# K's high part one slot later on ScalarE, its low part one slot later on VectorE

## The chip, the cores and the metric

The kernel runs on one core of one Trainium2 chip, in one launch. The metric is the device time of that core in microseconds. The kernel before takes 1835.96 us (median of 3 runs, 1834.97 to 1836.04).

## The reference

Inputs are x (16 batches of 512 rows by 512), a context of 16 x 512 x 1024, a length for each batch, two scalar gates, a bias row, and the weights of eight experts. All is fp32. Cut to what matters:

```
k, v  = split(ctx, 2, axis=2)                      # each 16 x 512 x 512
q     = heads(layernorm(x), 16) * 32 ** -0.5       # 16 heads of 32
s     = einsum('bhqd,bhkd->bhqk', q, heads(k)) + b + mask by length
x     = x + tanh(g_xattn) * (softmax(s) @ heads(v))
h     = layernorm(x)
logit = cos(h, centroids) + h @ w_route            # 8 experts, the best 2 kept
x     = x + tanh(g_ffn) * sum_e gate_e * (gelu(h @ w1_e + b1_e) @ w2_e + b2_e)
```

## The kernel before

There are two parts. The attention, which the change touches, comes first and fills the span up to about 1270 us; the experts' blocks follow.

The attention is a loop over 64 groups, written out in full. A group is one batch and four of its heads (a batch is four groups, g = 0 to 3). The loop is a software pipeline: in step l several groups are under way at once, each in another stage. A step has 16 slots, s = 0 to 15, and each engine's program is an in-order list of what it does in slot 0, slot 1 and so on. Engines meet only at semaphores.

**What TensorE does in a slot.** First "QK" (line 899): one 128x512 tile of the logits of group l, into one of two banks. Then "M" (line 911): a tile of the same logits, turned, of group l+2, whose only use is the row maximum. In some slots more follows:
- slot 0 and slot 3: the transposes TQ and TK of Q and K of group l+3 (`turn_rows`, line 858);
- slots 5, 9 and 13, and slot 1 of the next step: four heads' products of probabilities with V (`values`, line 830). The one in slot 5 is the first product with V. Slot 2 of the next step: the row sums (line 844);
- slot 5, behind the product: the transposes MT of the maxima of group l+1 (line 866);
- slots 7 and 9: the transposes DT of the row sums and OT of the output of group l-1 (line 932);
- slots 10 and 14: XT and LG, for the router.

**What the others do.** ScalarE takes each QK bank with an exponential (line 755), one a slot; QK of slot s waits for the exponential of slot s-2. VectorE takes each M bank with a maximum (line 1167), one a slot; M of slot s waits for the maximum of slot s-2. GpSimd adds up probabilities.

**The two turn banks.** All transposes go into two PSUM banks, `psT[0]` and `psT[1]`, in a fixed order: list `TURNS` (line 110) numbers them, and even numbers use bank 0, odd ones bank 1. In a full step the order is TQ, SM (the row sums), TK, MT, DT, OT, XT, LG, so TQ, TK, DT and XT share one bank, and SM, MT, OT and LG the other. `put_turn` (line 371) makes TensorE wait until the former user of the bank is taken out, `take_turn` (line 377) makes the taker wait for the transposes.

**Q and K in two parts.** Q and K are split into a high part in the matmul's format and the remainder. For Q (side 0) and K (side 1) `evac_turned` (line 703, ScalarE, line 708) copies the turn bank to the high part; `lo_part` (line 1082, VectorE, line 1086) subtracts the high part from the bank, gives the low part and releases the bank. SyncE then places them: two copies of the high part and one of the low part for each side, 256 KB each (line 464), and behind them the turned maxima, after ScalarE has copied those in slot 6 (`take_maxima`, line 727; DMA line 527). TensorE waits for all of them in slot 0 of the next step.

Before the change, K's transposes TK stand in slot 3 on TensorE, the high part in slot 4 behind that slot's exponential, the low part in slot 5 behind that slot's maximum. In steps with g = 0 ScalarE also normalises Q of a later batch, in slots 7, 9, 12 and 14 (line 697).

Of the kernel before, what the change touches and what calls it, by code (L numbers as in the profile page):

```python
# [142 lines left out]
def flamingo_kernel(nc, x, ctx_in, lens, g_xattn, g_ffn, b_in, w1, b1, w2, b2, cent, w_route, out):  # L143
# [31 lines left out]
    with outer:  # L175
# [54 lines left out]
        with ExitStack() as ctx:  # L230
# [146 lines left out]
            def take_turn(eng, st, name, off=0):  # L377

                i, before = turn_of(st, name, off)
                eng.wait_ge(s_turn[i], before + 1)  # L380
                return psT[i], s_took[i]
# [59 lines left out]
            def prob_of(st, off, u):  # L441


                return prob[:, u if u >= 2 else (st.l + off + u) % 2, :, :]
# [227 lines left out]
            def _(act):  # L672
# [30 lines left out]
                def evac_turned(st, side):  # L703

                    if st.rnd is not None or st.l + 3 >= 1:
                        act.wait_ge(s_stk[side], st.count(48, 3, 0))
                    bank, took = take_turn(act, st, "TK" if side else "TQ")
                    act.activation(turnedH[:, side, :], bank[:, :], ACT.Copy).then_inc(s_full, 1)
# [25 lines left out]
                def step(st):  # L734
                    if st.l == -1:
                        take_maxima(st)
                        i, before = turn_of(st, "MT")
                        act.wait_ge(s_took[i], before + 1)
                        for t in range(2):
                            act.dma_start(stB[98 + t:99 + t, 0, :, :].bitcast(F32),  # L740
                                          mT[HG * t:HG * t + HG, :].bitcast(F32)).then_inc(s_md[0], 16)
                    for s in range(16):
                        u, j = s // 4, s % 4
                        if st.on(0):
                            if j == 0 and st.l >= 1:


                                act.wait_ge(s_pv, st.count(PV, -1, (2, 1, 3, NT)[u]))
                                if u in (0, 2):
                                    act.wait_ge(s_acc, st.count(ADDS, -1, ADDS if u else HG))  # L750
                                else:
                                    i, before = turn_of(st, "SM")
                                    act.wait_ge(s_turn[i], before + 1)
                            act.wait_ge(s_qk, st.count(16, 0, s + 1))
                            act.activation(prob_of(st, 0, u)[:, j, :], psS[j % 2][:, :], ACT.Exp).then_inc(s_exp, 1)  # L755
                        if s in (0, 4) and st.on(3):
                            evac_turned(st, s // 4)
                            if s == 4 and st.l < 0:
                                place_k(st)
                        if s == 6 and st.on(1) and st.l >= 0:  # L760
                            take_maxima(st)
                        if s in (0, 4) and st.l == G:
                            for e in ((0, 1), (2, 3))[s // 4]:
                                w2_hi(e)
                        if s == 2 and st.on(-1):

                            act.wait_ge(s_pv, st.count(PV, -1, NT))
                            if st.l >= 2:
                                b, before = turn_of(st, "OT", -1)
                                act.wait_ge(s_turn[b], before + 1)  # L770
                            act.activation(attT[:, :], psO[:, :], ACT.Copy).then_inc(s_out, 1)
                        if s == 3 and st.on(-1):
                            if st.l >= 2:
                                b, before = turn_of(st, "DT", -1)
                                act.wait_ge(s_turn[b], before + 1)
                            bank, took = take_turn(act, st, "SM")
                            act.activation(sumT[:, :], bank[:, :], ACT.Copy).then_inc(took, 1)
                        if s == 8 and st.on(-5) and st.l <= G:
                            normalise(st)
                        if s == 11 and st.on(-5) and st.l <= G:  # L780
                            bank, took = take_turn(act, st, "XT")
                            act.activation(xT[:, :, :].rearrange("p k t -> p (k t)"), bank[:, :], ACT.Copy).then_inc(took, 1)
                        if st.g() == 0 and s in (7, 9, 12, 14) and st.on(4):
                            normalise_q(st, (7, 9, 12, 14).index(s))
                        if s == 10 and st.g() == 1 and st.on(-6) and st.l <= G:
                            gate_exp(st)
# [212 lines left out]
            def _(dve):  # L999
# [151 lines left out]
                def step(st):  # L1151
# [9 lines left out]
                    for s in range(16):  # L1161
                        if st.on(2):

                            if s == 0 and st.l + 2 >= 1:
                                dve.wait_ge(s_nm, st.count(2, 2, 0))
                            dve.wait_ge(s_m, st.count(16, 2, s + 1))
                            dve.tensor_reduce(mx[:, s // 4, s % 4:s % 4 + 1], psM[s % 2][:, :], AX.X, ALU.max).then_inc(s_mx, 1)  # L1167
                        if s == 0 and st.on(-6) and st.l <= G:
                            route_logit(st, s)
                        if s in ((1, 2) if st.l == -1 else (1, 5)) and st.on(3) and st.l != -2:  # L1170
                            lo_part(st, int(s > 1))
                        if s in (5, 6, 12, 13, 14, 15) and st.g() == 1 and st.on(-6) and st.l <= G:
                            route(st, s)
                        late = 10 if st.l in (-2, -1) else 0
                        if st.g() in (2, 3) and s - late in (0, 3) and st.on(8 - st.g()):
                            stats(st, 2 * (st.g() - 2) + (s - late) // 3)
                        if st.g() in (2, 3) and s - late in (2, 4) and st.on(8 - st.g()):
                            aggregate(st, 2 * (st.g() - 2) + (s - late) // 4)
                        if s == 8 and st.on(-1):

                            bank, took = take_turn(dve, st, "DT")
                            sums = bank[:, :].rearrange("p (i h c) -> p i h c", i=NT, h=HG)[:, :, :, 0]
                            dve.reciprocal(rsum[:, :, :], sums).then_inc(took, 1)
                        if s == 10 and st.on(-1):

                            b, before = turn_of(st, "DT")
                            dve.wait_ge(s_took[b], before + 1)
                            i, before = turn_of(st, "OT")
                            dve.wait_ge(s_turn[i], before + 1)
                            each = rsum[:, :, :].rearrange("p i (h a) -> p (i h) a", a=1).to_broadcast([P, NT * HG, DH])  # L1190
                            heads = psT[i][:, :].rearrange("p (h c) -> p h c", c=DH)
                            dve.tensor_tensor(heads, heads, each, ALU.mult).then_inc(s_scaled, 1)
                        if s == 11 and st.on(-1):
                            g, par = st.g(-1), ((st.l - 1) // 4) % 2
                            if g == 0:
                                dve.wait_ge(s_res[par], st.bpair(16, -1, 16))
                            dve.wait_ge(s_scaled, st.count(1, -1, 1))
                            bank, took = take_turn(dve, st, "OT")
                            dst = xres[:, par, :, g * P:(g + 1) * P]
                            dve.scalar_tensor_tensor(out=dst, in0=bank[:, :].rearrange("p (i c) -> p i c", i=NT), scalar=tanh_a[:, 0:1],  # L1200
                                                     in1=dst, op0=ALU.mult, op1=ALU.add).then_inc(took, 1)
                        if s == 10 and st.g() == 1 and st.on(-5) and st.l <= G:
                            row_norms(st)
                        if s in (12, 13) and st.on(-1):
                            column_stats(st, 2 * (s - 12))
                        if s == 14 and st.g() == 0 and st.on(-4):
                            row_stats(st)
                        if s == 15 and st.on(-5) and st.l <= G:
                            route_logit(st, s)
# [449 lines left out]
```

## Time and profile before

| | |
|---|---|
| median of 3 runs | 1835.96 us |
| profiled execution: time, span | 1835.64 us, 1833.9 us |
| granted TensorE clock, mean of the span | 0.988 of full speed |
| TensorE matmul busy | 1732.6 us, 94% |
| VectorE busy | 1360.4 us, 74% |
| GpSimd busy | 1231.4 us, 67% |
| ScalarE busy | 1190.3 us, 65% |
| maxima on VectorE (line 1167) | 1024 of 690 ns |
| exponentials on ScalarE (line 755) | 1024 of 597 ns |
| QK (line 899), M (line 911) on TensorE | 1024 each, 467 and 416 ns |

"Busy" counts the time in which an engine has an instruction under way. Neighbouring instructions overlap a little in the records, so the distance from start to start is what an instruction costs its queue, and its own duration is what a waiting engine has to sit out. A row of the timeline gives the start, the duration, engine and line; "x3" is three instructions merged into one row; in brackets stands how long the engine was idle before and what ended the wait.

### The profile page before, as it was taken

Reading aid. Unit: us, or ns where it says so; the run is one execution under the profiler, and the core shown is the slowest. Engines: PE = TensorE matmul, PEld = TensorE weight load, DVE = VectorE, ACT = ScalarE, POOL = GpSimd, SP = SyncE. Lnnn points to the kernel's source line nnn. Section 1 sums busy time; section 2 is a strip of 40 time slices with the busy share of each in tenths; the row PEclk is TensorE's granted clock in tenths of the full one; section 3 lists DMA queues with packets and bytes.
Section 4 is the critical chain, followed back from the end, with each engine's and each line's share of the span. In section 5 each row is a group of like instructions: output and inputs, shape, how many; then the busy total and the mean of one; then the engine's idle time right before and its main releaser. Section 6 shows DMA issues by size and latency. Waiting matters only on the chain. (4 is left out here: it accounts for less than half of the span.)

```text
span 1833.9 us, 33174 instructions
## 1 busy us (share of the span) xinstructions
PE 1732.6 (94%) x9754; PEld 1047.6 (57%) x9755; DVE 1360.4 (74%) x3003; ACT 1190.3 (65%) x2049; POOL 1231.4 (67%) x1399
## 2 busy tenths in 40 slices
PE   2889999999999999999999999999699999999997
PEld 1344555555555555555554555554578778777886
DVE  5767888878888778788787877872566776767765
ACT  4457677676776767767677677766356666666664
POOL 1348567585775857757666676664568888888886
PEclk9999999999999999999999999999699999999999
DMA  7879899898998989989989897874458788887784
GB/s 156 143 133 188 163 172 187 128 214 146 171 185 130 210 150 171 186 128 206 155 164 191 138 199 106 182 128 144 143 121 170 152 161 159 177 156 150 155 165 74
DMA packets 173099, 291.45 MB, mean 159 GB/s; under 512 B 38014, under 2 KB 42110, under 8 KB 172976
## 3 DMA queue, kind: packets, MB, share of 16 engines
q1 hardware_dynamic: 138704, 219.88, 61.6%
q0 software_dynamic: 32960, 67.68, 18.7%
q10 hardware_dynamic: 1312, 2.38, 1.1%
q8 instruction: 61, 1.00, 0.3%
q14 instruction: 62, 0.51, 0.1%
HBM read 127.09 MB, written 71.63 MB: 108 GB/s over the span
## 5 line engine op out<-in xcount | busy, mean ns | idle before, releaser
L1167 DVE TENSOR_REDUCE bank<-bank 128x1 f32<-128x512 f32 x1024 | 695.9, 690 | 246.0 <-PE bank L911 237.8
L755 ACT ACTIVATE prob<-bank 128x512 f32<-128x512 f32 x1024 | 593.1, 597 | 363.7 <-PE bank L899 362.8
L659 POOL TENSOR_TENSOR prob<-prob 128x512 f32<-128x512 f32 x252 | 315.9, 1295 | 325.3 <-PE bank L830 325.3
L899 PE MATMUL bank<-stB,stack_a_then_w_hi 100*128 100x512 f32 x1024 | 476.9, 467 | 20.4 <-ACT prob L755 13.7
L911 PE MATMUL bank<-stack_a_then_w_hi,stB 98*128 98x512 f32 x1024 | 423.4, 416 | 23.5 <-DVE bank L1167 11.5
L899 PEld LDWEIGHTS bank<-stB,stack_a_then_w_hi 100*128 100x128 f32 x1024 | 193.5, 189 | 253.8 <-ACT prob L755 175.6
L663 POOL TENSOR_TENSOR prob<-prob 128x512 f32<-128x512 f32 x252 | 315.5, 1296 | 0.0
L830 PE MATMUL bank<-prob,vin 128*32 128x512 f32 x2048 | 273.6, 606 | 0.7 <-ACT prob L755 0.7
L1439 POOL DMA_INDIRECT out_dram<-yout,scatter_ids x144 | 227.7, 1581 | 52.5 <-issue 39.0
L911 PEld LDWEIGHTS bank<-stack_a_then_w_hi,stB 98*128 98x128 f32 x1024 | 198.1, 194 | 74.2 <-DVE bank L1167 42.2
L1412 POOL DMA_INDIRECT rows_in<-xn_rows,gather_ids x152 | 179.1, 1178 | 59.4 <-issue 44.3
L1373 PE MATMUL bankb<-turned_parts,w_parts 128*128 128x512 f32 x888 | 218.8, 402 | 0.0
L1373 PE MATMUL bankb<-stack_a_then_w_hi,gelu_parts 128*128 x576 | 198.8, 406 | 0.4
L1373 PEld LDWEIGHTS bankb<-turned_parts,w_parts 128*128 128x128 f32 x888 | 165.9, 190 | 37.8
L1545 ACT ACTIVATE yout<-out_with_bias,row_gates 128x512 f32<-128x512 f32 x144 | 92.3, 712 | 78.7 <-DVE out_with_bias L1619 68.0
L1565 DVE TENSOR_TENSOR turned_parts<-bankb,turned_parts 128x512 fp32r<-128x512 f32 x148 | 95.2, 684 | 54.2 <-ACT turned_parts L1525 48.0
L1373 PEld LDWEIGHTS bankb<-stack_a_then_w_hi,gelu_parts 128*128 128x128 f32 x576 | 108.2, 188 | 29.0 <-issue 4.8
L844 PE MATMUL bank<-prob,ones 128*32 128x512 f32 x1040 | 124.8, 598 | 0.0
L1373 PE MATMUL bankb<-regrouped_then_w,gelu_parts 128*128 x288 | 114.3, 397 | 0.0
L1525 ACT ACTIVATE turned_parts<-bankb 128x512 fp32r<-128x512 f32 x148 | 81.3, 596 | 40.5 <-PE bankb L1459 20.3
L1553 ACT ACTIVATE gelu<-bankb,b1s 128x512 f32<-128x512 f32 x74 | 50.9, 688 | 84.6 <-PE bankb L1373 65.4
L858 PE MATMUL bank<-ident,regrouped_then_w 128*128 128x128 f32 x512 | 81.0, 283 | 22.7 <-ACT regrouped_then_w L697 21.7
(205 smaller groups left out, 2177.5 us busy)
## 6 DMA issues: line engine op xcount, KB each, us to landing
stB<-regrouped_then_w SPq DMA_DIRECT2D x192, 256.0 KB, 5.7
stack_a_then_w_hi<-regrouped_then_w SPq DMA_DIRECT2D x183, 256.0 KB, 6.4
x_k_then_w<-in_x_dram SPq DMA_DIRECT2D x16, 1024.0 KB, 7.9
x_k_then_w<-in_ctx_dram SPq DMA_DIRECT2D x16, 1024.0 KB, 11.6
vin<-in_ctx_dram SPq DMA_DIRECT2D x16, 1024.0 KB, 8.4
xres<-in_x_dram SPq DMA_DIRECT2D x16, 1024.0 KB, 6.4
out_dram<-xres SPq DMA_DIRECT2D x16, 1024.0 KB, 7.4
xn_rows<-xn SPq DMA_DIRECT2D x60, 256.0 KB, 5.5
```

The source lines that it names most:

```text
L659: pool.tensor_tensor(first[:, j, :], first[:, j, :], more[:, j, :], ALU.add).then_inc(s_acc, 1)
L663: pool.tensor_tensor(first[:, j, :], first[:, j, :], then[:, j, :], ALU.add).then_inc(s_acc, 1)
L755: act.activation(prob_of(st, 0, u)[:, j, :], psS[j % 2][:, :], ACT.Exp).then_inc(s_exp, 1)
L830: last = pe.matmul(psO[DH * j:DH * (j + 1), :], vin[:, vpar, kt, c0:c0 + DH], p[:, j, :], start=(u == 0), stop=(u == NT - 1), skip_group_c ...
L844: last = pe.matmul(bank[DH * j:DH * (j + 1), :], ones[:, 0:DH], p[:, j, :], start=(u == 0), stop=(u == NT - 1), skip_group_check=True, til ...
L899: pe.matmul(psS[j % 2][:, :], stA[0:100, g, j, kt * P:(kt + 1) * P], stB[0:100, g, j, :], start=True, stop=True).then_inc(s_qk, 1)
L911: pe.matmul(psM[s % 2][:, :], stB[0:98, g, j, i * P:(i + 1) * P], stA[0:98, g, j, :], start=True, stop=True).then_inc(s_m, 1)
L1167: dve.tensor_reduce(mx[:, s // 4, s % 4:s % 4 + 1], psM[s % 2][:, :], AX.X, ALU.max).then_inc(s_mx, 1)
L1373: last = pe.matmul(bank, wts(p), mov(q), start=start and i == 0, stop=stop and i == 2)
L1412: pool.indirect_dma_start(rows[:, par, c, :], None, xn_d, bass.IndirectOffsetOnAxis(ap=gids[:, par, c:c + 1], axis=0), bounds_check=TOK - ...
L1439: pool.indirect_dma_start(out_rows, bass.IndirectOffsetOnAxis(ap=sids[:, h, c:c + 1], axis=0), yout[:, h, c, :], None, bounds_check=TOK - ...
L1565: dve.tensor_tensor(xTb[:, 1, k, :], bank_of(st, USE[k])[:, :], xTb[:, 0, k, :].bitcast(F32), ALU.subtract).then_inc(f_use, 1)
```

## The change

ScalarE's copy of K's high part goes from slot 4 to slot 5 and stands behind the exponential of slot 5. VectorE's subtraction for K's low part goes from slot 5 to slot 6 and stands behind the maximum of slot 6. In the steps before group 0, ScalarE's own DMAs for K move along with the copy. Nothing else moves: TensorE's, GpSimd's and SyncE's lists stay, and so do the order of the turn banks and all waits.

```diff
-                        if s in (0, 4) and st.on(3):
-                            evac_turned(st, s // 4)
-                            if s == 4 and st.l < 0:
+                        if s in (0, 5) and st.on(3):
+                            evac_turned(st, s // 5)
+                            if s == 5 and st.l < 0:
                                 place_k(st)
...
-                        if s in ((1, 2) if st.l == -1 else (1, 5)) and st.on(3) and st.l != -2:
+                        if s in ((1, 2) if st.l == -1 else (1, 6)) and st.on(3) and st.l != -2:
                             lo_part(st, int(s > 1))
```

## Rows read from the trace of the kernel before

**Rows 1.** Busy time by stage, the attention without its first two steps.
```profile
116.00:1270.00 1154.00, 1128.41 (x6797) 588.68 (x6800) 908.86 (x2107) 810.54 (x1471) 769.96 (x1040) 1.00 0.87 165
```

**Rows 2.** Groups of instructions by line, from 116 to 1215 us.
```profile
L899 PEld LDWEIGHTS bank<-stB,stack_a_then_w_hi 100*128 100x128 f32 x931 | 175.5, 189 | 218.9 <-ACT prob L755 154.3 <-issue 53.6
```

**Rows 3.** Timeline of TensorE, slots 6 to 9 of step 30 (g = 2).
```profile
649.30 0.48 PE L899 MATMUL bank<-stB,stack_a_then_w_hi 100*128 100x512 f32 x1
649.62 0.39 PE L911 MATMUL bank<-stack_a_then_w_hi,stB 98*128 98x512 f32 x1
649.85 0.39 PE L899 MATMUL bank<-stB,stack_a_then_w_hi 100*128 100x512 f32 x1
650.08 0.40 PE L911 MATMUL bank<-stack_a_then_w_hi,stB 98*128 98x512 f32 x1
650.32 0.60 PE L932 MATMUL bank<-ident,regrouped_then_w 128*128 128x128 f32 x4
650.67 0.48 PE L899 MATMUL bank<-stB,stack_a_then_w_hi 100*128 100x512 f32 x1
650.99 0.39 PE L911 MATMUL bank<-stack_a_then_w_hi,stB 98*128 98x512 f32 x1
651.41 0.50 PE L899 MATMUL bank<-stB,stack_a_then_w_hi 100*128 100x512 f32 x1
651.75 0.40 PE L911 MATMUL bank<-stack_a_then_w_hi,stB 98*128 98x512 f32 x1
652.08 0.64 PE L830 MATMUL bank<-prob,vin 128*32 128x512 f32 x4
```

**Rows 4.** Timeline of VectorE, slots 5 to 8 of the same step.
```profile
648.57 0.67 DVE L1167 TENSOR_REDUCE bank<-bank 128x1 f32<-128x512 f32 x1
649.14 0.68 DVE L1086 TENSOR_TENSOR regrouped_then_w<-bank,regrouped_then_w 128x512 fp32r<-128x512 f32 x1
650.05 2.07 DVE L1167 TENSOR_REDUCE bank<-bank 128x1 f32<-128x512 f32 x3 [0.23 <-PE bank L911]
```

**Rows 5.** Timeline of ScalarE, slots 4 to 8 of the same step.
```profile
647.92 0.59 ACT L708 ACTIVATE regrouped_then_w<-bank 128x512 fp32r<-128x512 f32 x1
648.40 0.60 ACT L755 ACTIVATE prob<-bank 128x512 f32<-128x512 f32 x1
649.82 0.60 ACT L755 ACTIVATE prob<-bank 128x512 f32<-128x512 f32 x1 [0.81 <-PE bank L899]
650.31 0.57 ACT L727 ACTIVATE regrouped_then_w<-bank 8x512 fp32r<-8x512 f32 x1
650.79 1.08 ACT L755 ACTIVATE prob<-bank 128x512 f32<-128x512 f32 x2
```

**Rows 6.** Timeline of TensorE, transposes OT of step 29 and QK behind them.
```profile
633.94 0.66 PE L932 MATMUL bank<-ident,regrouped_then_w 128*128 128x128 f32 x4
634.35 0.48 PE L899 MATMUL bank<-stB,stack_a_then_w_hi 100*128 100x512 f32 x1
```

**Rows 7.** Timeline of all engines, slots 7, 8 and 12 of step 28 (g = 0).
```profile
611.85 0.60 PE L932 MATMUL bank<-ident,regrouped_then_w 128*128 128x128 f32 x4
...
612.80 1.33 ACT L697 ACTIVATE regrouped_then_w<-x_k_then_w,q_shift,rstd 128x512 f32<-128x512 f32 x1
...
613.91 0.64 ACT L755 ACTIVATE prob<-bank 128x512 f32<-128x512 f32 x1
...
617.41 0.50 PE L899 MATMUL bank<-stB,stack_a_then_w_hi 100*128 100x512 f32 x1 [0.77 <-ACT prob L755]
```

**Rows 8.** Timeline of SyncE's DMA issues from slot 4 of step 30 on.
```profile
648.54 1.85 SPq L464 DMA_DIRECT2D stack_a_then_w_hi<-regrouped_then_w  x3
650.90 1.32 SPq L527 DMA_DIRECT2D stB<-regrouped_then_w  x2
...
659.50 1.13 SPq L502 DMA_DIRECT2D stack_a_then_w_hi<-bias_mask_rows  x4
```

**Rows 9.** DMA issues by size and median us to landing, 648.5 to 650.5 us.
```profile
stack_a_then_w_hi<-regrouped_then_w SPq DMA_DIRECT2D x3, 256.0 KB, 7.3
```

## The prediction

> **What bounds the kernel now.** I read the busy times by stage first. In the attention TensorE is busy 1128.41 of 1154 us, at a granted clock of 1.00, while VectorE has 908.86 and ScalarE 810.54 [rows 1]. So a step costs what TensorE's list costs, and the two engines that the change touches have room on average. The groups by line say where TensorE is held at all: the weight loads of QK sit idle 154.3 us in front of exponentials over 931 instructions, 0.17 us each [rows 2]. Last I read the timelines of one step, slot by slot, because the change is a matter of order and an average says nothing on that. Step 30 is a plain one (g = 2); its order and distances in slots 6 to 9 repeat from step to step, so it stands for the steps with g = 1, 2 and 3.
>
> In slots 6 to 9 TensorE runs QK, M, QK, M, DT, QK, M, QK, M, product [rows 3]. Up to DT the starts are 0.23 to 0.32 us apart: nothing holds it. DT starts at 650.32. The low part of K, which frees DT's bank, ran from 649.14 to 649.82 [rows 4], 0.50 us ahead. That half microsecond is all the cover there is.
>
> **What the ScalarE move does.** Before: exponential of slot 4, high part at 647.92, exponential of slot 5 at 648.40 [rows 5]. After: the exponential of slot 5 takes the place at about 647.92 and the high part follows at about 648.40 and ends at 648.99, 0.48 us later. The cost on ScalarE is nothing: the same two instructions in the other order, and the next exponential, of slot 6, waited 0.81 us for TensorE [rows 5]. The gain is nothing too: the earlier exponential releases QK of slot 7 only, which ran at 649.85 [rows 3], when the exponential had been done since 649.00 [rows 5]. No wait of TensorE in slots 4 to 7 goes.
>
> **What the VectorE move does.** The low part stood in a pause of VectorE: it ended at 649.82 and the maximum of slot 6 waited another 0.23 us for M [rows 4]. That maximum needs M of slot 6, so its start at 650.05 can't be earlier. The low part now queues behind it. From the row before, a subtraction starts 0.57 us after the maximum ahead of it (648.57 to 649.14), the three maxima in one row come 0.69 apart (2.07 / 3) [rows 4]; I take 0.60. Start 650.65, end 650.65 + 0.68 = 651.33. A release takes about 0.03 to 0.05 us more: the exponential of slot 7 ended at 650.79 + 0.60 = 651.39 and QK of slot 9, which waits for it, started at 651.41 [rows 3, 5]. DT therefore starts at about 651.38 and not 650.32: TensorE stands still for 1.06 us, in order, with QK of slot 8 and all that follows behind DT. Bounds: 1.03 with the 0.57, 1.17 with the 0.69 and the larger release.
>
> **What comes back in the same step.** From DT to the second product TensorE took 652.08 - 650.32 = 1.76 us. One gap in it is a wait: M of slot 8 to QK of slot 9 took 0.42 (650.99 to 651.41), for the exponential of slot 7, which stood behind the turned maxima at 650.31 [rows 3, 5]. After the stall that exponential is long done, so the two pairs run at 0.32 and 0.24 to 0.33. DT to QK is 0.35 when nothing held the transposes, and 0.41 where they start behind a pause [rows 3, 6]. I take 0.41 + 0.32 + 0.24 + 0.24 + 0.33 = 1.54, a return of 0.22 us. M of slot 9 now needs the maximum of slot 7, which follows the low part and ends near 651.23 + 0.69 = 651.92; M of slot 9 would start by TensorE's own list at 651.38 + 0.41 + 0.32 + 0.24 + 0.24 = 652.59, so that is not late. Net 1.06 - 0.22 = 0.84 us per plain step. Bounds: 0.70 (return of 0.33) and 1.17 (no return).
>
> Behind the second product ScalarE and VectorE have caught up in either kernel, so the rest of the step is the same, 0.84 us later, and nothing absorbs it.
>
> **Steps with g = 0.** There ScalarE is the one that is late: its normalising of Q runs from 612.80 for 1.33 us, the exponential of slot 8 starts at 613.91 behind it, and QK of slot 12 still waits 0.77 us for an exponential [rows 7]. With the stall DT starts at 611.85 + 1.06 = 612.91, QK of slot 8 at 613.32 and ends 0.48 later at 613.80, still ahead of 613.91. ScalarE's chain does not move, so the 0.84 us is given back by slot 12. I take 0 for these steps; the upper bound is the whole 0.84, if VectorE and not ScalarE sets the pace behind slot 9 once the low part has moved.
>
> **Transfers.** On SyncE the high parts are issued 0.48 us later, the low part once it is there, near 651.4, and the turned maxima behind it, near 652.0 and not 650.90. K's three copies needed 7.3 us to land [rows 8, 9]: from the last issue at about 649.8 that is 657.1, against the next step at 659.5 [rows 8]. With the low part 1.6 us later it lands at 658.7, against 659.5 + 0.84 = 660.3. That hides 1.6 us of slack and no more; I count 0. GpSimd's additions wait for exponentials and products that don't move and cost nothing.
>
> **The sum.** The stall needs a K in slot 6 (steps up to 60) and a DT in slot 7 (steps from 1): 60 steps. 15 of them have g = 0 (4, 8, ... 60), 45 don't. 45 x 0.84 + 15 x 0 = 37.8 us. The profiled execution took 1835.64 us, 0.32 below the median, so I compare with it: 1835.64 + 37.8 = 1873.4 us, slower by 2.1%.
>
> **The Trainium skill on the clock.** The granted clock is 1.00 over the stretch although TensorE idles for 1154 - 1128.41 = 25.6 us in it, some of it in waits of 0.77 us [rows 1, 7]. The Trainium skill (TensorE: Matmul & The Clock Gate, Part 1) says that the throttled state is the default and that activity is what releases it. By that, the added idle could cost clock as well as time; that case is a rival below, and without it the sum stands. No row of this kernel shows idle of 1 us per step bringing the clock down.
>
> **Rivals.**
> 1. The stall is there and the placed rows come too late on top, or the g = 0 steps don't give it back. The low part's slack of 1.6 us is for a step without bulk loads; with a megabyte load in the queue a landing could slip. For it: DMA busy share 0.87 [rows 1]. Against it: what is loaded in bulk is issued behind these rows in most steps. Price: the full 1.06 in all 60 steps, 63.6 us, 1899 us.
> 2. More comes back than I see, as the plain steps have waits for exponentials behind slot 9 too: 154.3 us over about 58 steps is 2.7 us per step [rows 2]. If a third of each stall is absorbed there and only 0.55 stays: 45 x 0.55 = 24.8, 1860 us. Against it: the pause of the second product empties both queues.
> 3. The other side, faster: the exponential of slot 5 runs 0.48 us earlier, and if the release of DT were not what K's low part holds, the chain of exponentials could run ahead. It would take away the wait in front of QK of slot 9, 0.42 - 0.24 = 0.18 us [rows 3], in 60 steps: 10.8 us, 1824.8 us. It decides if DT's bank is free by 650.32 and the exponential of slot 7 can start before 650.79; but the latter stands behind QK of slot 7 and the turned maxima, which don't move.
> 4. No change: the two turn banks are counted so that DT doesn't follow K's transposes in its bank. Then both moves are in cover, 1835.6 us. The order of the turns speaks against it: K's and DT's are two apart in every step.
> 5. The clock falls, as said above: a tenth of the stretch at 1.2 GHz would add up to 0.1 x 1128 = 113 us, 1986 us with the stall.
>
> **How the numbers follow.** Forecast (net 0.70 to 1.06 per plain step, small change in g = 0 steps: 1867 to 1888) 0.72; rival 1 0.11; rival 2 0.11; rival 3 0.02; rival 4 0.02; rival 5 0.02. The range that leaves out no more than 2 in 10 reaches a good way into rivals 1 and 2: 1860 to 1892. What a measurement of this kernel can tell from no change is about 0.2%, 3.7 us; rivals 1, 2 and 5 are slower with the forecast: slower 0.96, same 0.02, faster 0.02.
>
> **What would show it.** In the timeline of a plain step: the low part of K behind the maximum of slot 6, its start about 0.6 us after it; idle time of TensorE before DT (line 932), ended by VectorE's line 1086, near 1 us, where no such releaser stood before; about 60 of them, some 60 us in the list of waits. QK of slot 6 to DT 2.08 us instead of 1.02 [rows 3]; DT to the second product near 1.54 instead of 1.76. Plain steps 0.84 us longer, and the step with g = 0 as long as before. The waits of QK for exponentials should shrink by some 10 us in slot 9 and more in g = 0 steps. It is wrong if no wait stands in front of DT, if waits for DMA appear in slot 0, or if the granted clock leaves 1.00.

## The result and the profile after

The changed kernel takes 1880.21 us (median, 1878.3 to 1882.68) against 1835.47 us for the kernel before in the same session: ratio 1.0244, 95% interval 1.0231 to 1.0256, 44.7 us slower. 1873.4 us was forecast, in a range of 1860 to 1892. The profiled execution took 1879.62 us, its span 1877.9 against 1833.9.

The list of waits of the changed kernel (engine, what waited, who released it: us in total, times, longest):
```profile
PEld bank L899 <- ACT prob L755: 128.9, 205, 0.9
PEld bank L932 <- ACT regrouped_then_w L727: 84.7, 60, 1.4
...
PE bank L932 <- DVE regrouped_then_w L1086: 60.5, 60, 1.0
```

The third row is new: 60 waits of TensorE in front of DT (line 932), ended by VectorE's low part (line 1086), 1.0 us each. The first row is the other side: in the list of before, the same weight loads waited 175.6 us in 280 waits for exponentials, now 128.9 in 205. The second row is the same 60 stalls seen by the weight loads, with another name: ScalarE's copy of the turned maxima. That copy counts up the semaphore of the other turn bank, but DT needs a count there that was reached before. The name is a guess of the profile from the last event, not a cause: in the kernel before, DT started at 650.32 when that copy had only just started, at 650.31 [rows 3, 5], and a run below moves the copy without moving DT.

TensorE in the changed kernel, slots 5 to 9 of step 30, the step of [rows 3]:
```profile
670.77 0.60 PE L866 MATMUL bank<-ident,regrouped_then_w 128*8 128x128 f32 x4
671.12 0.48 PE L899 MATMUL bank<-stB,stack_a_then_w_hi 100*128 100x512 f32 x1
671.44 0.39 PE L911 MATMUL bank<-stack_a_then_w_hi,stB 98*128 98x512 f32 x1
671.67 0.40 PE L899 MATMUL bank<-stB,stack_a_then_w_hi 100*128 100x512 f32 x1
671.91 0.40 PE L911 MATMUL bank<-stack_a_then_w_hi,stB 98*128 98x512 f32 x1
673.31 0.63 PE L932 MATMUL bank<-ident,regrouped_then_w 128*128 128x128 f32 x4 [1.00 <-DVE regrouped_then_w L1086]
673.69 0.48 PE L899 MATMUL bank<-stB,stack_a_then_w_hi 100*128 100x512 f32 x1
674.01 0.40 PE L911 MATMUL bank<-stack_a_then_w_hi,stB 98*128 98x512 f32 x1
674.25 0.40 PE L899 MATMUL bank<-stB,stack_a_then_w_hi 100*128 100x512 f32 x1
674.49 0.40 PE L911 MATMUL bank<-stack_a_then_w_hi,stB 98*128 98x512 f32 x1
674.82 1.07 PE L830 MATMUL bank<-prob,vin 128*32 128x512 f32 x8
```

From QK of slot 6 to DT it is 673.31 - 671.12 = 2.19 us; before it was 1.02 [rows 3]. So the stall is 1.17. The 1.00 in brackets is less, because it counts only from the end of M of slot 7, and before the change DT started while that M still ran. Behind DT the second pair follows the first at once: M of slot 8 to QK of slot 9 takes 0.24 where it took 0.42.

VectorE in the same step, against [rows 4]:
```profile
671.87 0.70 DVE L1167 TENSOR_REDUCE bank<-bank 128x1 f32<-128x512 f32 x1 [0.81 <-PE bank L911]
672.48 0.68 DVE L1086 TENSOR_TENSOR regrouped_then_w<-bank,regrouped_then_w 128x512 fp32r<-128x512 f32 x1
673.08 0.69 DVE L1167 TENSOR_REDUCE bank<-bank 128x1 f32<-128x512 f32 x1
```

The maximum of slot 6 now sits idle 0.81 us, where it was 0.23: the low part left that pause empty and stands behind it. The low part starts 0.61 us after the maximum and ends at 673.16; DT starts 0.15 later.

The attention as a whole, with the columns of [rows 1] (length, busy time of TensorE, its weight loads, VectorE, ScalarE and GpSimd, then the granted clock, here 1.00):
```profile
116.00:1315.00 1199.00, 1124.50 (x6792) 585.87 (x6791) 904.28 (x2107) 817.03 (x1470) 769.21 (x1040) 1.00 0.82 159
```

Starts of MT in steps 28, 29 and 30 (g = 0, 1, 2), before:
```profile
610.47 0.60 PE L866 MATMUL bank<-ident,regrouped_then_w 128*8 128x128 f32 x4
...
629.82 0.60 PE L866 MATMUL bank<-ident,regrouped_then_w 128*8 128x128 f32 x4
...
648.94 0.60 PE L866 MATMUL bank<-ident,regrouped_then_w 128*8 128x128 f32 x4
```

and after, in steps 28 and 29 (that of step 30 is the first row of TensorE's timeline above, at 670.77):
```profile
631.12 0.60 PE L866 MATMUL bank<-ident,regrouped_then_w 128*8 128x128 f32 x4
...
650.74 0.60 PE L866 MATMUL bank<-ident,regrouped_then_w 128*8 128x128 f32 x4
```

The step with g = 0 took 19.35 us and takes 19.62, 0.27 more; the one with g = 1 took 19.12 and takes 20.03, 0.91 more. Steps with g = 2 and 3 take 19.51 and 19.52 where they took 18.59 and 18.58. 45 x 0.91 + 15 x 0.27 = 45.0, against a span that is 44.0 longer.

### The profile page after: what moved, and what is told of

It is laid out like the page before. It is cut to its first block and busy times, and to the rows that moved or that the text cites. A ratio compares the mean times of both kernels' runs of the same rounds, so it can differ in the third digit from the quotient of the medians.

```text
span 1877.9 us, 33174 instructions
## 1 busy us (share of the span) xinstructions
PE 1728.1 (92%) x9754; PEld 1044.1 (56%) x9755; DVE 1355.9 (72%) x3003; ACT 1197.4 (64%) x2049; POOL 1229.9 (65%) x1399
## 5 line engine op out<-in xcount | busy, mean ns | idle before, releaser
L899 PE MATMUL bank<-stB,stack_a_then_w_hi 100*128 100x512 f32 x1024 | 471.2, 461 | 7.5 <-DMA stB<-regrouped_then_w 4.4
L899 PEld LDWEIGHTS bank<-stB,stack_a_then_w_hi 100*128 100x128 f32 x1024 | 193.8, 190 | 218.8 <-ACT prob L755 128.9
L932 PEld LDWEIGHTS bank<-ident,regrouped_then_w 128*128 128x128 f32 x512 | 53.9, 140 | 139.6 <-ACT regrouped_then_w L727 84.7
```

Of the source, the lines that this page charges most:

```text
L899: pe.matmul(psS[j % 2][:, :], stA[0:100, g, j, kt * P:(kt + 1) * P], stB[0:100, g, j, :], start=True, stop=True).then_inc(s_qk, 1)
L932: last = pe.transpose(bank[:, i * P:(i + 1) * P], src[:, i * P:(i + 1) * P], ident[:, :])
```

## The experiments

The reference time in each is that of the kernel before, on the same chip in the same session.

**The high part alone.**
```diff
-                        if s in (0, 4) and st.on(3):
-                            evac_turned(st, s // 4)
-                            if s == 4 and st.l < 0:
+                        if s in (0, 5) and st.on(3):
+                            evac_turned(st, s // 5)
+                            if s == 5 and st.l < 0:
```


> Only ScalarE's high part of K moves, from slot 4 to slot 5; VectorE's low part stays in slot 5. My theory (the whole loss is the release of DT's bank by VectorE) expects no change: 1835.5 us, within 3 us, and no wait in front of DT. A rival, that the later high part pushes the low part and the maximum of slot 6, would give 0.2 us or more in each of 60 steps, 1847 us or more.

Measured: 1834.88 us, ratio 0.9995 (0.9986 to 1.0005). ScalarE's move costs and gives nothing. In its waits the low part sits idle 19.4 us for the high part, in 35 waits; 14.3 us of it, in 4 waits, stood in the kernel before. What is new, about 5 us in 31 waits, fits into VectorE's pause and reaches nobody.

**The low part alone.**
```diff
-                        if s in ((1, 2) if st.l == -1 else (1, 5)) and st.on(3) and st.l != -2:
+                        if s in ((1, 2) if st.l == -1 else (1, 6)) and st.on(3) and st.l != -2:
```


> Only VectorE's low part of K moves, from slot 5 to slot 6; ScalarE's high part stays in slot 4. My theory expects all of the loss: 1880 us, 60 waits of 1.0 us in front of DT, ended by VectorE. The rival that both moves share the loss expects well under 1880, about 1868.

Measured: 1880.93 us, ratio 1.0242 (1.0226 to 1.0257), and the same 60 waits:
```profile
PE bank L932 <- DVE regrouped_then_w L1086: 60.4, 60, 1.0
```

All of the loss is here.

**The low part in slot 6 where g = 0 only.**
```diff
-                        if s in ((1, 2) if st.l == -1 else (1, 5)) and st.on(3) and st.l != -2:
+                        if s in ((1, 2) if st.l == -1 else (1, 6 if st.g() == 0 else 5)) and st.on(3) and st.l != -2:
```


> The low part moves to slot 6 in the 15 steps with g = 0 alone, the rest is the kernel before. By the step lengths of the changed kernel these steps lose 0.26 us each (0.86 in the first ones): about 5 us, 1840.5 us. If ScalarE absorbed everything, as I predicted, 1835.5 us; if nothing were absorbed there, 15 x 0.92, 1849 us.

Measured: 1839.73 us, ratio 1.0021 (1.0012 to 1.0030), 4.1 us over the reference of 1835.61. Its waits show 15 of 1.0 us in front of DT:
```profile
PE bank L932 <- DVE regrouped_then_w L1086: 15.1, 15, 1.0
```

15.1 us of waiting cost 4.1 us of time: about three quarters are given back, not all.

**The low part one slot later still.** From the changed kernel:
```diff
-                        if s in ((1, 2) if st.l == -1 else (1, 6)) and st.on(3) and st.l != -2:
+                        if s in ((1, 2) if st.l == -1 else (1, 7)) and st.on(3) and st.l != -2:
```


> The changed kernel with the low part behind the maximum of slot 7, one slot later still. DT is released one maximum later, 0.69 us. My theory, a stall in front of DT with nothing behind it that absorbs, expects 0.69 us more in each of 60 steps: 41 us on top of 1880, 1921 us, and waits of 1.7 us in front of DT. If the loss came from the moved work's place among the maxima and not from DT's wait, it would stay near 1880 us.

Measured: 1938.46 us, ratio 1.0554 (1.0538 to 1.0570), 58 us over the changed kernel and not 41. The wait in front of DT is 98.9 us in 60, 0.64 us more each where 0.69 was expected. The expected time was missed all the same: 38 of the 58 us are these waits. The rest shows in the busy time by stage (columns as above), for the attention, for the 8 us from slot 7 of step 28 (g = 0) on, for a part of them, and for DT's surroundings in the next step:
```profile
116.00:1375.00 1259.00, 1146.88 (x6780) 596.19 (x6772) 904.57 (x2105) 817.92 (x1466) 768.56 (x1040) 0.98 0.78 152
658.70:666.90 8.20, 6.60 (x32) 3.50 (x30) 4.41 (x8) 6.41 (x10) 8.20 (x7) 0.79 1.05 193
661.60:665.10 3.50, 3.50 (x14) 1.15 (x14) 1.55 (x3) 3.00 (x4) 3.50 (x4) 0.51 1.05 127
680.40:685.00 4.60, 2.80 (x18) 1.25 (x17) 3.28 (x8) 2.70 (x6) 4.60 (x5) 1.00 1.04 151
```

The granted clock falls to its lower level, 1.2 GHz, in the first of the two steps and holds in the second. TensorE in the first step and, from 682.66 on, in the second:
```profile
660.73 0.63 PE L932 MATMUL bank<-ident,regrouped_then_w 128*128 128x128 f32 x4 [1.60 <-DVE regrouped_then_w L1086]
...
662.63 1.93 PE L830 MATMUL bank<-prob,vin 128*32 128x512 f32 x8
664.50 0.91 PE L932 MATMUL bank<-ident,regrouped_then_w 128*128 128x128 f32 x4
...
682.66 0.63 PE L932 MATMUL bank<-ident,regrouped_then_w 128*128 128x128 f32 x4 [1.80 <-DVE regrouped_then_w L1086]
...
684.17 1.06 PE L830 MATMUL bank<-prob,vin 128*32 128x512 f32 x8
685.17 0.66 PE L932 MATMUL bank<-ident,regrouped_then_w 128*128 128x128 f32 x4
```

The product takes 1.93 us and not 1.06, the transposes OT 0.91 and not 0.66. The second step held its clock though its idle stretch was the longer one, 1.80 us against 1.60. A step in which the clock falls is about 1.5 us longer than its like; there are 16 in this trace, which is 24 us, about what the span, 63.1 us longer than that of the changed kernel, has over the longer waits (63.1 - 60 x 0.64 = 24.7).

**The changed kernel, DT in slot 8.**
```diff
-                        if s in (7, 9) and st.on(-1):
-                            name, src = ("DT", sumT) if s == 7 else ("OT", attT)
-                            if s == 7:
+                        if s in (8, 9) and st.on(-1):
+                            name, src = ("DT", sumT) if s == 8 else ("OT", attT)
+                            if s == 8:
...
-                        if s == 8 and st.on(-1):
+                        if s == 9 and st.on(-1):
                             bank, took = take_turn(dve, st, "DT")
```


> The changed kernel, with the transposes DT one slot later on TensorE (slot 8, behind QK and M of that slot) and their reciprocal in slot 9. The low part stays in slot 6. If the loss is DT's wait for its bank, QK and M of slot 8 now run inside it: the wait shrinks from 1.0 to about 0.5 us, the second product comes 0.46 us later than before the change and not 0.92, about 1856 us. If the loss were the low part's place in VectorE's queue, 1880 us.

Measured: 1855.29 us, ratio 1.0109 (1.0094 to 1.0125). More than half of the loss goes, though the low part stands where the change put it. The second product comes 0.44 us later than before the change (3.58 us behind MT against 3.14), close to the 0.46 expected. The size of the remaining wait was not met: 11.0 us in 60, 0.18 each, and not 0.5:
```profile
661.48 0.63 PE L932 MATMUL bank<-ident,regrouped_then_w 128*128 128x128 f32 x4 [0.18 <-DVE regrouped_then_w L1086]
```

QK and M of slot 8 are not at their full pace there. They wait for the exponential and the maximum of slot 6, which end at 660.42 and 660.75, start at 660.47 and 660.81, and so fill more of the wait than I took. DT itself starts 2.54 us behind MT, as in the changed kernel.

**Control: the kernel before with DT in slot 8.** The same edit.

> Control for the run above: the kernel before with the same move of DT to slot 8. QK of slot 9 waits for the exponential of slot 7 in either order, so DT only fills that wait: no change, 1835.5 us within 4.

Measured: 1839.14 us, ratio 1.0018 (1.0009 to 1.0027), 3.3 us slower: DT's move costs a little by itself, 0.1 us in a plain step. Why is open. With DT in slot 8 the late low part costs 1855.3 - 1839.1 = 16.2 us, with DT in slot 7 44.7.

**The turned maxima copied in slot 7, in the kernel before.**
```diff
-                        if s == 6 and st.on(1) and st.l >= 0:
+                        if s == 7 and st.on(1) and st.l >= 0:
                             take_maxima(st)
```


> The kernel before, with ScalarE's copy of the turned maxima moved from slot 6 to slot 7, behind that slot's exponential. If the 0.25 us that came back behind DT in the changed kernel was the wait of QK of slot 9 for the exponential of slot 7, held up by this copy, then the kernel before gains it here: 0.25 us in 45 plain steps, about 1824 us. If the return had another cause, 1835.5 us.

Measured: 1826.53 us, ratio 0.9952 (0.9939 to 0.9966), 9.3 us faster than the kernel before. TensorE in slots 7 to 9 of one step:
```profile
646.39 0.60 PE L932 MATMUL bank<-ident,regrouped_then_w 128*128 128x128 f32 x4
646.75 0.48 PE L899 MATMUL bank<-stB,stack_a_then_w_hi 100*128 100x512 f32 x1
647.07 0.40 PE L911 MATMUL bank<-stack_a_then_w_hi,stB 98*128 98x512 f32 x1
647.30 0.39 PE L899 MATMUL bank<-stB,stack_a_then_w_hi 100*128 100x512 f32 x1
647.53 0.44 PE L911 MATMUL bank<-stack_a_then_w_hi,stB 98*128 98x512 f32 x1
647.90 1.07 PE L830 MATMUL bank<-prob,vin 128*32 128x512 f32 x8
```

DT to the product is 1.51 us where it was 1.76 [rows 3], and M of slot 8 to QK of slot 9 0.23 where it was 0.42. No stall was needed for it. The 9.3 us are not 45 x 0.25: steps with g = 2 and 3 get 0.2 us shorter, those with g = 1 only 0.06, and those with g = 0 from step 8 on stay as they were; the rest comes from the first steps.

**The same move in the changed kernel.** The same edit.

> The changed kernel with the same move of the turned maxima to slot 7. There the stall in front of DT already gives the exponential of slot 7 its time, so the theory expects nothing: 1880 us within 3. If the move helped by itself, 1869 us.

Measured: 1880.93 us, ratio 1.0247 (1.0231 to 1.0262): nothing, on 1880.21. What this copy holds up is free already behind the stall. Its list of waits names the 60 stalls another way, and the timeline shows why:
```profile
PE bank L932 <- ACT regrouped_then_w L727: 60.3, 60, 1.0
```
```profile
672.01 0.68 DVE L1086 TENSOR_TENSOR regrouped_then_w<-bank,regrouped_then_w 128x512 fp32r<-128x512 f32 x1
672.14 0.57 ACT L727 ACTIVATE regrouped_then_w<-bank 8x512 fp32r<-8x512 f32 x1
672.83 0.63 PE L932 MATMUL bank<-ident,regrouped_then_w 128*128 128x128 f32 x4 [1.00 <-ACT regrouped_then_w L727]
```

The copy now ends 2.41 us behind MT, where it ended 1.93 behind it in the changed kernel; that is 0.02 after the low part, so the profile takes it for the releaser. DT starts 2.54 behind MT in both. The name has changed with the copy's place, the time has not; in the code DT still waits for the low part.

**The low part in slot 7, DT in slot 8.** The two edits together.

> K's low part behind the maximum of slot 7, and DT in slot 8. With the low part in slot 7 and DT in slot 7 the time was 1938.5 us, some 19 more than its 60 longer waits explain (60 x 0.65 = 39 on 1880); its trace shows 16 steps 1.5 us too long, with the granted clock at 0.95 to 0.98 where it was 1.00. If that excess is the clock, which falls when TensorE stands idle for 1.6 to 1.8 us at once, then here, where QK and M of slot 8 cut each idle stretch to about 1.2 us, the excess is gone: 1855.3 + 39 = 1894 us and a clock of 1.00. If the excess has another cause in the late low part (transfers, VectorE), it stays: about 1914 us.

Measured: 1890.73 us, ratio 1.0298 (1.0282 to 1.0314): the excess is gone, and so is the fall of the clock. Its attention, and DT of one plain step:
```profile
116.00:1320.00 1204.00, 1141.25 (x6770) 584.05 (x6773) 906.57 (x2106) 814.04 (x1464) 769.16 (x1040) 1.00 0.82 159
```
```profile
678.56 0.63 PE L932 MATMUL bank<-ident,regrouped_then_w 128*128 128x128 f32 x4 [0.78 <-DVE regrouped_then_w L1086]
```

The waits in front of DT are 49.3 us in 60, 0.8 us in a plain step and at most 1.0, less than the 1.2 expected. Against the run with DT in slot 8 and the low part in slot 6 it is 35.4 us more, 0.59 for each of 60 steps; the low part starts 0.60 later behind MT, one maximum by its start-to-start distance.

**The turned maxima in slot 8, in the kernel before.**
```diff
-                        if s == 6 and st.on(1) and st.l >= 0:
+                        if s == 8 and st.on(1) and st.l >= 0:
                             take_maxima(st)
```


> The kernel before with the copy of the turned maxima in slot 8 on ScalarE, one slot later than in the run that gave 1826.5 us. The wait of QK of slot 9 is gone in both, and OT in slot 9 needs the copy only after the second product. The theory expects the same 1826.5 us within 3; if the later rows or the next slot's exponential then come late, it lies above 1830 us.

Measured: 1825.60 us, ratio 0.9945 (0.9932 to 0.9959). The same as slot 7 within the intervals, and both beat both kernels.

## Why the prediction held, step by step

**The cover.** That the low part had half a microsecond of cover in front of DT and lost it is shown: the low part alone gives all of the loss, its move by one more slot adds 0.64 us to each wait, and DT's move to a later slot takes more than half of the loss away.

**ScalarE's move, nothing.** Shown by the run with it alone, 0.9995.

**The stall, 1.06 us.** The mechanism was right, the size 0.11 short: 1.17 measured. I took 0.60 from the maximum to the low part (0.61 measured), 0.68 for the low part, and 0.05 for the release, from an exponential that releases QK. The low part's end releases DT 0.15 us later. That is where the 0.1 is; why this pair takes longer is open. The upper bound was added up wrongly too: with 0.69 and 0.05 it comes to 650.05 + 0.69 + 0.68 + 0.05 - 650.32 = 1.15, not 1.17, so the measured stall lies just above it.

**The return, 0.22 us.** 1.76 us from DT to the second product became 1.51 (674.82 - 673.31), a return of 0.25. The cause is shown by the pair of runs with the maxima moved: 9.3 us gained in the kernel before, none in the changed one. Net 0.92 per plain step and not 0.84, within the bounds of 0.70 to 1.17.

**Steps with g = 0, nothing.** This term failed in part: 0.27 us each by the step lengths, 4.1 us by the run with these steps alone. The upper bound had the right place. ScalarE's chain moves by less than 0.1 us up to slot 12, as I worked out. But VectorE's queue behind the second product is paced by its own work. M of slot 10, the maxima of slots 10 and 11 and M of slot 13 in step 28 of the kernel before (MT at 610.47):
```profile
615.33 0.40 PE L911 MATMUL bank<-stack_a_then_w_hi,stB 98*128 98x512 f32 x1
615.76 0.70 DVE L1167 TENSOR_REDUCE bank<-bank 128x1 f32<-128x512 f32 x1 [1.35 <-PE bank L911]
616.97 0.69 DVE L1167 TENSOR_REDUCE bank<-bank 128x1 f32<-128x512 f32 x1
618.22 0.39 PE L911 MATMUL bank<-stack_a_then_w_hi,stB 98*128 98x512 f32 x1
```

TensorE from slot 12 on and VectorE from slot 10 on in the same step of the changed kernel (MT at 631.12):
```profile
638.15 0.50 PE L899 MATMUL bank<-stB,stack_a_then_w_hi 100*128 100x512 f32 x1
638.49 0.40 PE L911 MATMUL bank<-stack_a_then_w_hi,stB 98*128 98x512 f32 x1
638.72 0.42 PE L899 MATMUL bank<-stB,stack_a_then_w_hi 100*128 100x512 f32 x1
639.28 0.50 PE L911 MATMUL bank<-stack_a_then_w_hi,stB 98*128 98x512 f32 x1
```
```profile
637.33 0.70 DVE L1167 TENSOR_REDUCE bank<-bank 128x1 f32<-128x512 f32 x1 [1.11 <-PE bank L911]
637.94 0.69 DVE L1192 TENSOR_TENSOR bank<-bank,rsum 128x512 f32<-128x512 f32 x1
638.53 0.69 DVE L1167 TENSOR_REDUCE bank<-bank 128x1 f32<-128x512 f32 x1
```

QK of slot 12 starts 7.03 us after MT, before it was 617.41 - 610.47 = 6.94: the stall is given back by slot 12. Then M of slot 13 waits until 639.28 for the maximum of slot 11, which ended at 638.53 + 0.69 = 639.22 and stands behind the scaling of the output (line 1192). This row of VectorE's work starts with the maximum of slot 10, which came with the stall: 6.21 us behind MT, before it was 5.29. In the kernel before, the maximum of slot 11 had ended at 617.66, 0.56 ahead of M of slot 13; that cover was too short for the stall. The third product stands 8.59 us behind MT where it stood 8.07, 0.52 later. About half of this returns by TQ of the next step (11.99 against 11.69), which before started 0.05 us after ScalarE's normalising (line 697) had ended. I had read ScalarE's queue to the end of the step and VectorE's only to slot 9.

**Transfers, nothing.** The waits for DMA in slot 0 stay at two steps at the start of the kernel (on QK 4.4 us in total for the matmuls and 5.2 for their weight loads; 5.3 and 6.0 before).

**The sum.** With the measured terms it is 45 x 0.92 + 15 x 0.27 = 45.5 us, against 44.7 measured and 37.8 forecast. The forecast lacked 45 x 0.08 = 3.6 us in the plain steps, most of it the release, and 15 x 0.27 = 4.1 us in the steps with g = 0. Both errors went the same way, so neither hid the other.

**The rivals.** Rival 1 is out (1899 us, no late transfers, most of the stall in the g = 0 steps given back). Rival 2 is out: nothing is absorbed behind the second product in plain steps. Rivals 3 and 4 are out with the run of the high part alone and the 60 waits. But rival 3's price was real: the 0.18 us in front of QK of slot 9, which I valued at 10.8 us, is gained by moving the turned maxima. Rival 5, the clock, is out for this change (1.00 in the attention) and came true, at a smaller size, when the stalls became longer: 0.98 over the attention and about 24 us.

## What to carry to other kernels

An instruction that reads a bank also releases it. Before it is moved into a "pause" further on, look for who takes the bank next and how long before that the release stands now; here it was 0.50 us of cover and the next instruction on the queue was 0.6 us long. A pause that a product makes for VectorE and ScalarE stands between the slot's last maximum and the next slot's; behind the next slot's maximum it is over. Where a stall in one place gives something back, the returned time names a wait that can be taken out without the stall.

## What the runs showed of the hardware

In the run with the low part in slot 7 and DT in slot 7, TensorE stood idle for 1.6 to 1.8 us in front of DT in each of 60 steps. In 16 of them the clock fell to the lower of its two levels, 1.2 GHz, between 0.1 us before and 1.7 us after DT's start (mean granted clock 0.98 over the attention, 0.92 over the long step shown, 657.59 to 679.33, and 0.79 in the 8.2 us shown). In the other 44 it held, also behind a stretch of 1.80 us. The length of the one stretch therefore doesn't decide; what picks the 16 steps is open. With idle stretches of 1.0 us in the changed kernel, and of 0.8 to 1.0 us with the low part in slot 7 and DT in slot 8, the clock stayed at 1.00. The Trainium skill (TensorE: Matmul & The Clock Gate, Part 1) has the throttle released by activity and back without it. The traces agree in so far as the clock fell, behind the first two steps of the attention, only in the run with the longest idle stretches.

A release by VectorE's subtraction reached TensorE's transposes 0.15 us after its recorded end in all 60 stalls of the changed kernel (673.16 to 673.31). It is not VectorE as such: a maximum reached M after 0.06 us (639.22 to 639.28). A release by ScalarE's exponential reached QK after 0.05 us in the kernel before; the exponential of slot 7 in [rows 5] ended by its own record at 651.36, not at the 651.39 that I worked out from the merged row, and QK of slot 9 started at 651.41 [rows 3].
